# Two set-up steps move off VectorE: the context's normalisation to ScalarE, the second attention's gated output weights to GpSimd

## What is computed

```
m = silu(cond) @ w_ada + b_ada            # nine vectors of 256: shift, scale, gate, three times
h = ln(x) * (1 + sc_msa) + sh_msa
x = x + (self_attn(h) @ w_so + b_so) * g_msa                    # windows of 128 rows, 16 heads      stage A
h = ln(x) * (1 + sc_mca) + sh_mca
x = x + (topk_cross_attn(h, ctx) @ w_co + b_co) * g_mca         # the 16 largest of 77 scores        stage B
h = ln(x) * (1 + sc_mlp) + sh_mlp
x = x + swiglu(h) * g_mlp                                       #                                    stage C
xq, xkv = ada_ln(x, cond, Wss_q), ada_ln(ctx, cond, Wss_kv)     # normalised over the 256 channels
out = x + attention(xq @ Wq, xkv @ Wkv) @ Wp                    # cross attention over 77 rows       stage D
```

## Time and profile before

| | |
|---|---|
| median of 3 runs | 980.44 us (979.55 to 982.67) |
| profiled execution | 981.46 us, of which the span of the profile is 979.7 us |
| busy: TensorE, VectorE, ScalarE, GpSimd | 95%, 89%, 76%, 72% of the span |
| instructions | 32584 |

### The profile page before, as it was taken

One profiled execution on the slowest core, in us unless ns is written; L12 is line 12 of the kernel. 1 busy time (PEld: TensorE's weight loads), 2 busy tenths in 40 slices (PEclk: granted clock), 3 DMA queues, 4 the chain that ended last, 5 costly groups with the idle time before them and its releaser, 6 DMA issues. The chain is left out here.

```text
span 979.7 us, 32584 instructions
## 1 busy us (share of the span) xinstructions
PE 932.0 (95%) x10500; PEld 809.7 (83%) x10500; DVE 868.1 (89%) x4318; ACT 744.6 (76%) x1604; POOL 701.1 (72%) x1099
## 2 busy tenths in 40 slices
PE   6987899999999999999999999999999999998996
PEld 3775788888888898888888888888888898777884
DVE  2569999999999999999999999999999999897633
ACT  2355788888878888888888888888888887687764
POOL 1226867887777788787777778878777777666752
PEclk9779999999999999999999999999999999999998
DMA  8276200123333332223333333222333333210000
GB/s 289 62 150 135 67 18 18 26 65 77 72 73 76 77 78 51 63 64 68 77 71 72 77 77 73 46 68 65 71 78 70 73 78 71 46 33 7 7 7 18
DMA packets 210555, 66.44 MB, mean 68 GB/s; under 512 B 188520, under 2 KB 200961, under 8 KB 209746
## 3 DMA queue, kind: packets, MB, share of 16 engines
q1 hardware_dynamic: 210386, 64.35, 29.6%
HBM read 39.02 MB, written 25.30 MB: 66 GB/s over the span
## 5 line engine op out<-in xcount | busy, mean ns | idle before, releaser
L2344 PE MATMUL ps<-hT_C,w_m_sb 128*128 128x128 f32 x2048 | 256.6, 278 | 1.9 <-DVE hidden_C L1674 1.5
L2344 PEld LDWEIGHTS ps<-hT_C,w_m_sb 128*128 128x128 f32 x2048 | 243.6, 192 | 14.4 <-issue 8.2
L1043 ACT ACTIVATE silu_C<-ps,cols_sb 128x128 f32<-128x128 f32 x256 | 93.6, 366 | 121.8 <-PE ps L2344 109.9
L2355 PE MATMUL ps<-w_m_sb,hidden_C 128*128 128x256 f32 x512 | 121.1, 380 | 0.2
L1580 DVE MATCH_REPLACE8 scores_left_B<-mx_B,scores_left_B 128x77 f32<-128x77 f32 x512 | 108.3, 224 | 0.0
L1576 DVE MATCH_REPLACE8 scores_left_B<-mx_B,scores_B 128x77 f32<-128x77 f32 x512 | 108.1, 224 | 0.0
L2355 PEld LDWEIGHTS ps<-w_m_sb,hidden_C 128*128 128x128 f32 x512 | 92.7, 190 | 10.9 <-DVE hidden_C L1674 0.7
L666 POOL TENSOR_TENSOR scores_D<-scores_D,mx_D 128x616 f32<-128x616 f32 x62 | 76.0, 1226 | 25.0 <-DVE mx_D L1647 24.9
L661 POOL TENSOR_TENSOR p_B<-scores_B,mx_B 128x616 f32<-128x616 f32 x64 | 78.5, 1227 | 19.6 <-DVE mx_B L1574 19.0
L1674 DVE SCALAR_TENSOR_TENSOR hidden_C<-ps,cols_sb,silu_C 128x128 f32<-128x128 f32 x256 | 83.6, 337 | 9.7 <-ACT silu_C L1043 9.5
L701 POOL TENSOR_TENSOR p_D<-scores_D,rc_D 128x616 f32<-128x616 f32 x63 | 77.0, 1225 | 10.9 <-DVE rc_D L1625 5.4
(11 more groups left out here) (188 smaller groups left out, 2439.7 us busy)
## 6 DMA issues: line engine op xcount, KB each, us to landing
p_turned_D<-p_blocks_D SPq DMA_DIRECT2D x200, 80.0 KB, 2.4
pT_D<-p_turned_D SPq DMA_DIRECT2D x50, 320.0 KB, 3.5
xn_turned_A<-xn_blocks_A SPq DMA_DIRECT2D x124, 32.0 KB, 2.0
xn_A<-xn_turned_A SPq DMA_DIRECT2D x31, 128.0 KB, 2.1
x_A<-in_x SPq DMA_DIRECT2D x28, 128.0 KB, 2.4
out<-y_D SPq DMA_DIRECT2D x28, 128.0 KB, 2.1
w_m_sb<-in_w_m SPq DMA_DIRECT2D x3, 1024.0 KB, 5.2
w_mod_sb<-in_w_mod SPq DMA_DIRECT2D x2, 1024.0 KB, 9.9
```

The lines of the kernel that those rows point to most:

```text
L1043: sc.activation(SA[:, j, :], bank(f"C.up{j}")[:, 0:P], ACT.Silu, bias=col("bm1_a", j)).then_inc(sa_ok, 1)
L2344: ins = mm(bank(f"C.up{j}")[:, half * P:(half + 1) * P], w_m1[:, k, m:m + P], HT["C"][:, t % HT_COPIES["C"], k, :], start=(k == 0), stop=( ...
L2355: ins = mm(bank("C.dn0")[:, 0:CH], G[:, t % G_COPIES, j, :], w_m2[:, j, :], start=(j == 0), stop=(j == HJ - 1))
```

## The change

ScalarE gets `normalise_context()`, four activations with a scale and an offset for each row, behind `key_blocks(1)` and ahead of `set_up_values("B")` in its fill. Since an activation computes scale times input plus offset, GpSimd's `set_up_context_rstd()` works out the offset too (minus the mean, times the reciprocal root), which is two more instructions on 77x4 elements and two more waits of GpSimd for its own results. VectorE's `set_up_context()` goes. GpSimd gets `set_up_output_weights(1)`, the same two multiplications, behind `less_max(0, "B", 1)` and ahead of `add_bias(0, "B")`; it goes from VectorE's fill, where it stood between `maxima_a(2, 1)` and `add_maxima(2)`. `set_up_output_weights(0)` stays on VectorE.

```diff
+            cnm = sb("ctx_neg_mean", [LC, BATCH], F32, early)
@@ gpsimd
             def set_up_context_rstd():
                 pool.wait_ge(cstat, 2 * BATCH)
                 link(g.tensor_scalar(cve[:], cmv[:, :, 1], EPS1, None, ALU.add))
-                g.tensor_tensor(crs[:], cve[:], half_neg[0:LC, :], ALU.pow).then_inc(crstd, 1)
+                link(g.tensor_tensor(crs[:], cve[:], half_neg[0:LC, :], ALU.pow))
+                link(g.tensor_tensor(cnm[:], cmv[:, :, 0], neg_one[0:LC].to_broadcast([LC, BATCH]), ALU.mult))
+                g.tensor_tensor(cnm[:], cnm[:], crs[:], ALU.mult).then_inc(crstd, 1)
+
+            def set_up_output_weights(n):
+                pool.wait_ge(table_in[n], 32)
+                pool.wait_ge(ld["so"], 16 * 3)
+                pool.wait_ge(wo_done, n)
+                w = (w_so, w_co)[n]
+                for k in range(KC):
+                    ins = g.tensor_tensor(w_out["AB"[n]][:, k], w[:, k].unsqueeze(1).to_broadcast([P, BATCH, CH]),
+                                          gate[:, n], ALU.mult)
+                ins.then_inc(wo_done, 1)
@@ gpsimd, fill
                 less_max(0, "B", 1)
+                set_up_output_weights(1)
                 add_bias(0, "B")
@@ scalar
+            def normalise_context():
+                act.wait_ge(crstd, 1)
+                for b in range(BATCH):
+                    ins = sc.activation(ctxn[:, b, :], ctxn[:, b, :], ACT.Identity, scale=crs[:, b:b + 1], bias=cnm[:, b:b + 1])
+                ins.then_inc(cnorm, 1)
@@ scalar, fill
                 key_blocks(1)
+                normalise_context()
                 set_up_values("B")
@@ vector
-            def set_up_context():
-                dve.wait_ge(crstd, 1)
-                for b in range(BATCH):
-                    ins = v.tensor_scalar(ctxn[:, b, :], ctxn[:, b, :], cmv[:, b, 0:1], crs[:, b:b + 1],
-                                          ALU.subtract, ALU.mult)
-                ins.then_inc(cnorm, 1)
@@ vector, fill
                 set_up_modulation(2)
-                set_up_context()
                 set_up_output_weights(0)
@@ vector, fill
                 maxima_a(2, 1)
-                set_up_output_weights(1)
                 add_maxima(2)
```

## The result

| | before | changed |
|---|---|---|
| median | 980.44 us (5 runs, 979.54 to 982.67) | 987.08 us (5 runs, 984.73 to 990.84) |
| ratio, 95% interval | | 1.0064 [1.0036, 1.0093] |
| profiled execution | 981.46 us, span 979.7 us | 987.17 us, span 985.3 us |
| changed kernel in a second set of runs | 981.05 us (20 runs) | 987.14 us (6 runs), 1.0054 [1.0035, 1.0072] |

The forecast was 986.4 us. The single executions scatter more than the first three runs of before suggested. In the means of these two sets the loss is 6.3 us (standard error 1.2) and 5.5 us (0.7), together 5.7 us (0.6). The experiments brought 80 executions of before, with a mean of 982.05 us, against 986.87 us for the 11 of the changed kernel.

The account below looks back on a forecast made before the run. TensorE, busy 95% of the span, was taken as the bound, with fill delays passing through in order. Terms 5.28-0.84+1.5=5.9 us on 980.44 gave 986.4 us (chance 0.50), range 983.2 to 989.6.

Parts of the forecast that it names:

- Part 1: In the fill, moving the context's normalisation to ScalarE changes nothing: VectorE's 3.95 us become a wait for TensorE.
- GpSimd's pair: Two 128x1024 multiplications ahead of GpSimd's bias sum, from 74.84 us: 4.72 us, bounds 4.0 and 4.8.
- The collision: VectorE's `keep_chosen(0, 1)` meets GpSimd's second multiplication and delays its bias sum: 0.56 us, bounds 0 and 0.8.
- Won back: TensorE's waits vanish: 0.40 us for ScalarE's keys at `scores_a(2)`, 0.44 us for VectorE's `add_maxima(2)`.
- The sum at full clock: All engines behind the fill's stall move by 5.28-0.40-0.44=4.44 us, before any clock term.
- The clock: Falls to half inside TensorE's 5.3 us gap, slowing three steps behind it: +1.5 us, bounds 0 and +4.4.
- rival 2: Clock stays low to the end of `scores_t(2)` or longer: 8.8 us, 989.3 us; chance 0.15.
- The pipeline keeps the delay: Behind the fill, in-order lists carry a delay of TensorE, VectorE and GpSimd to the end unshortened.
- Rival 3: Delay is taken up later in TensorE's gaps up to about 118 us: about 982 us; chance 0.11.
- Rival 4: GpSimd's work is hidden, only VectorE's 0.44 us relief shows: 980.0 us; chance 0.05 with all unnamed gains.
- The base: Time of before to which the forecast's 5.9 us were added: the median of the runs, 980.44 us.

Follow-up runs that it names:

- part 1 alone: Against before, only the context's normalisation moved to ScalarE, both output weights kept on VectorE: ratio 0.9983, 980.88 us beside 983.05.
- weights only: Against before, only stage B's output weights moved to GpSimd, the context's normalisation left as it was: ratio 1.0048, 987.48 us.
- gap-filled: Changed kernel plus 10 unread matrix products on TensorE between stage D's keys and the late transposes: ratio 1.0033 to before, 986.16 us.
- changed again: The changed kernel run once more, unaltered, in a second set: ratio 1.0054 to before, 987.14 us.
- half on GpSimd: Changed kernel with only the first of the two multiplications on GpSimd, the second back on VectorE: ratio 1.0031 to before.
- the first with the early table: Changed kernel with stage B's tables spread earlier and GpSimd's pair moved up into its idle time: ratio 0.9974, 980.55 us beside 981.44 of before.
- gap filled again: Changed kernel plus 10 unread TensorE products, run once more on the changed kernel's chip: ratio 1.0061 to before, 986.20 us.
- late: Changed kernel with GpSimd's two multiplications behind its ten for stage B's values, tables as before: ratio 1.0005, 982.46 us beside 981.44 of before.

## Why the prediction was right, and where a term was off

The sum of the forecast was 5.9 us. It goes through the traces step by step.

- **Part 1, nothing: right.** VectorE's head start became 3.06 us of idle time, ScalarE's activations took 2.08 us within their cover, and the collision of GpSimd's reciprocal root with VectorE's products came as described: the two steps on 77x4 elements, 0.23 and 1.04 us in the trace of before, took 1.20 and 1.86 us, and GpSimd was still 1.37 us early for its next one. The kernel with part 1 alone has a stretch 0.06 us longer and a time 1.7 parts in a thousand lower. I had not forecast that gain, and no row within the touched steps explains it. A part of it may be the clock. In that set it spent 27.2 us at half clock against 30.6 (error 1.7), and the second low spell of the fill, from about 36 us on, differs by profile: 7 us long in the two kernels without part 1 (before, weights only), 3 to 3.5 us in six profiles with it, and absent in the other four. Twelve profiles don't show that part 1 is the cause.
- **GpSimd's pair, 4.72 us: right.** It took 4.65. The price worked out by columns was good to 2%. The estimate from the Trainium skill (GPSIMD Engine Reference, section "Elementwise — side-by-side cycle accounting"), 4.5, was 3% low.
- **The collision, 0.56 us: right.** The bias sum took 1.28 us instead of 0.73, so 0.55, and 0.72 in the kernel where the two don't meet. Both waited in turn as in the earlier trace rows. By the rule of the Trainium skill (SBUF — State Buffer, section "Who interferes with whom"), that a VectorE instruction with two SBUF inputs contends with a GpSimd instruction that reads SBUF for a port pair that only one can hold, the traces agree: VectorE's selection took 2.06 us in place of 0.80.
- **Won back, 0.40 and 0.44 us: right but for 0.18.** Behind the gap `scores_a(2)` follows the transposes without an idle time, and `add_maxima(2)` waits for TensorE instead of for VectorE's products. With the products early and the clock full, the 0.44 us are gone, but TensorE then waits 0.18 us for ScalarE at the same place; the whole stretch is 0.35 to 0.38 us shorter. That GpSimd's ten multiplications got shorter, 4.90 instead of 6.87 us, was worth little, as I had it: TensorE's wait ahead of `weigh_values(0, "B")`, put down to ScalarE in both traces, is 1.89 instead of 2.06 us.
- **The sum at full clock.** The forecast for the stretch was 5.28-0.84=4.44 us. I had taken it that the table lands as far ahead of the end of TensorE's keys as before, 1.91 us (74.84 against 76.75). In the gap-filled profile it landed 1.41 us ahead (71.82 against 73.23). That adds 0.5, and 4.94 stand against 4.98 measured.
- **The clock, +1.5 us: right in kind, off in size.** It fell inside the gap in all three profiles with a gap of 4.6 us or more (changed, changed again, weights only). But I had let it be back after three steps, and it stayed low for about 10 us in all three (in the changed kernel to 90.7 us, inside `project_v(3)`). The two profiles give 3.05 us, between my 1.5 and the 4.4 of rival 2, whose mechanism this is in the main. That the total still fits is luck: other differences between the two profiles cancel the excess. The changed kernel's had its clock back 3 us sooner (39.4 instead of 42.8 us) and was 1.3 us ahead at the end of the keys (75.45 against 76.75), and it lacked the low spell in the drain (0.65). 8.03-1.30-0.65=6.1, and small differences behind 92 us take 0.5 more, to the 5.6 us between the spans.
- **The pipeline keeps the delay: right.** 6.30, 6.25 and 6.49 us at three places over 750 us. Rival 3, that later gaps of TensorE take it up, falls with that. Rival 4 fell with the first row: the pair began when the DMA landed.
- **The base.** I took 980.44 us, the median of three runs, as the time of before. The means of its sets lie between 980.84 and 982.80 us, and the loss within a set is 5.7 us (error 0.6) rather than the 6.6 of the first two medians. A scatter of 18 to 43 us at half clock, which a single profile doesn't show, is what I hadn't allowed for.

## What to carry to other kernels

An engine that idles 28% of the span is no place for a step by that alone: look at what stands behind the new step in its list, and whether the engine next in line has slack at that very instant (here TensorE took GpSimd's result 0.05 us after it was made). The relief of the busiest engine is worth at most the wait that others have for it at that place, 0.44 of 2.57 us here. Before moving work to another engine, look for the load that it waits for: issued some 37 us sooner (30.4 instead of 67.7 us), the same step fits into idle time on either engine.

## What the runs showed of the hardware

- The time at half clock differs from one execution of the same kernel to the next by up to 25 us (18 to 43 us over 80 executions of before), and the time goes with it at 0.27 us for each. Between 36 and 39 us the clock was at its lower level in eight of the twelve profiles and full in four (both with the gap filled, half on GpSimd, the first with the early table), with the same list on TensorE up to there.
- An idle time of 1.91 us behind 4.5 us of dense products went with a fall of the clock, and one of 2.78 us with none. TensorE's wait of 1.89 us ahead of `weigh_values(0, "B")` was followed by a fall within 1.5 us of its end in four profiles (changed again, gap filled again, half, late), and by none in six with the same 1.89 us. The length of the gap alone doesn't decide it.
- While VectorE reads two tiles of SBUF and GpSimd reads SBUF, whole instructions take turns: 2.06 instead of 0.80 us on VectorE, 1.28 instead of 0.73 on GpSimd, and 1.20 for a GpSimd step of 0.23 us on 77x4 elements.
